# Attention heads on one Trainium2 core: ScalarE takes the second head's exponential of a cell ahead of the first head's

## The chip, the cores and the metric

The kernel runs on one core of a Trainium2 chip. A core has four compute engines that matter here: TensorE (PE in the profile; its weight loads are shown apart as PEld), VectorE (DVE), ScalarE (ACT) and GpSimd (POOL). SyncE (SP) issues transfers. Each engine takes its own list of instructions in order, and engines wait for each other on semaphores. The metric is device time in microseconds (us) of one execution.

## The reference, cut to what matters

The program is a whole block: feed-forward with experts, a wide attention, feed-forward again, a quantized linear layer, an attention with 16 heads, and the linear layer again. The change touches only the attention with 16 heads:

```
q = proj(Wq) / sqrt(DH);  k = proj(Wk);  v = proj(Wv)      # 4 batches, 16 heads, T = 1024, DH = 16
scores = einsum('bhid,bhjd->bhij', q, k)
dist = clip(i[:, None] - i[None, :], 0, 128)
scores = scores + rel[:, dist]                              # a bias by distance
scores = where(i >= j, scores, -inf)                        # causal
y = einsum('bhij,bhjd->bhid', softmax(scores), v)
out = x0 + y.reshape @ Wo.T
```

The bias differs from a constant only where a query lies less than 128 rows behind its key; that strip beside the diagonal, together with the causal mask, is called the band.

## The kernel before

**Units and cells.** The stage "heads" (function `attention_heads`) works through NU = 16 units: 4 batches by 4 groups of HG = 4 heads. A unit is 12 cells (list `CELLS`). A cell is one block j of 128 keys against one half c of the 1024 queries, cut by the causal mask, so that it is 128, 256, 384 or 512 queries wide. Nine of the 12 cells touch the band (`near_of`); they are called near cells here, and the three others, numbers 1, 4 and 7 counted from 0 and all 512 wide, far cells. Over the stage there are 144 near and 48 far cells.

**The four heads of a cell.** A cell has four positions, which hold heads 3, 0, 1 and 2 (`HEAD_OF`). For each position, PE multiplies keys by queries into a PSUM bank (L2316). In a near cell the band is then added: for head 3, at position 0, VectorE adds it in place (L2251); for the other three, PE adds it by two matmuls with an identity (L2320) right behind the score. ScalarE then takes the exponential from the bank into a tile `pt` (L2176). The row maximum is already in the score, as extra rows of the operand. In what follows score 0 to score 3 and exponential 0 to exponential 3 are those of the four positions, and "the add" is VectorE's band of position 0.

**Banks.** The scores of all positions share three PSUM banks in turn (`st_bank`, n % 3, where n counts positions through the stage). Before score n, PE waits until the exponential of n - 3 is done: score 3 of a cell takes the bank of position 0 of the same cell, and scores 0, 1 and 2 take those of positions 1, 2 and 3 of the cell before.

**Values.** The product with v (L2337, eight matmuls a cell) is issued two cells later, behind score 3 of the cell that is then current. It waits for all four exponentials of its own cell.

**What runs in between.** `heads_order` writes one list of steps by hand, and each engine walks it in that order. After each position's score it may place one piece of the row maxima of a later unit: score matmuls into three other banks (L2296) and VectorE's reductions (L2213, L2222, L2225). It also places steps of the next batch's projection (PE, ScalarE L1871 and L1874, VectorE L1903, GpSimd) and the end of the unit before (the transposes and the output projection, L2347, L2355, L2365). The maxima run 1.5 units ahead, so the last unit has none of them beside it. ScalarE has no list of its own: whatever stands in the common list between two positions, such as the projection's copies, stands in its queue there too.

Of the kernel before, what the change touches and what calls it, by code (L numbers as in the profile page):

```python
# [12 lines left out]
ACT = mybir.ActivationFunctionType  # L13
# [16 lines left out]
HG = 4  # L30
NHG = HEADS // HG
HP = HG - 1
# [78 lines left out]
def macaron(nc, x_d, wg_d, w13_d, w2_d, aq_d, ak_d, av_d, fw_d, fb_d, lq_d, lk_d, lv_d, lo_d,  # L111
            rel_d, gamma_d, beta_d, out_d):
    ctx = ExitStack()
    pe, act, dve, pool, sp = nc.tensor, nc.scalar, nc.vector, nc.gpsimd, nc.sync
    uid = [0]

    def sb(stack, name, shape, dt=F32):
        uid[0] += 1
        return stack.enter_context(nc.sbuf_tensor(f"{name}_{uid[0]}", shape, dt))
# [10 lines left out]
    with ctx:  # L130
# [39 lines left out]
        def act_root(at, n):  # L170
            act.wait_ge(*S("variance")(n))
            act.activation(sd[:, at], ve[:, at], ACT.Sqrt).then_inc(*S("root").up())
# [1886 lines left out]
        def attention_heads(tables, ahead):  # L2059
# [8 lines left out]
            NPT = 3 * HG  # L2068
# [4 lines left out]
            score, biased, exped, value, ys_ok = S("score"), S("biased"), S("exp"), S("value"), S("ys")  # L2073
# [16 lines left out]
            near_of = [min((c + 1) * BANK, (j + 2) * P) > max(j * P, c * BANK) for j, c in CELLS]  # L2090
            near_cells = [i for i in range(NCELL) if near_of[i]]

            with ExitStack() as st:
# [9 lines left out]
                pt = [sb(st, f"pt{i}", [P, BANK if i < 2 * HG else 3 * P]) for i in range(NPT)]  # L2103
# [11 lines left out]
                st_bank = lambda n: psum[:, 2 + n % 3, :]  # L2115

                def cell_of(i):

                    u, cell, pos = i
                    j, c = CELLS[cell]  # L2120
                    q0, q1 = max(j * P, c * BANK), (c + 1) * BANK
                    return (u * NCELL + cell) * HG + pos, j, c, HEAD_OF[pos], q0, q1, min(q1, (j + 2) * P)

                def stacks_of(r, u):
                    return S.dma(f"stack_in{r}")(2 * len(SLOTS) * (u // NR + 1))

                def on_sp():
                    for kind, i in order:
                        if kind == "qk" and i % (2 * KD * CB) == 0 and i // (2 * KD * CB) >= 2:
                            b = i // (2 * KD * CB)  # L2130
                            for u in range((b - 1) * NHG - NR, (b - 1) * NHG):
                                sp.wait_ge(*stacks_of(u % NR, u))
                        if kind == "load" and i >= NR:
                            sp.wait_ge(*score((i - NR + 1) * NCELL * HG))
                        ahead.on_sp(kind, i)
                        if kind == "max_out":
                            sp.wait_ge(*max_part(3 * i + 3))
                            sp.dma_start(m_scr[i % 2].rearrange("i c p -> c i p"),
                                         mparts[:, :, :]).then_inc(*S.dma("m_out").up())
                            sp.wait_ge(*S.dma("m_out")(i + 1))  # L2140
                            sp.dma_start(qs[i % NR][KS_ROWS:KS_ROWS + MROWS, :, :].rearrange("i h s -> i (h s)"),
                                         m_scr[i % 2].rearrange("i c p -> i (c p)")
                                         ).then_inc(*S.dma(f"m_in{i % 2}").up())
# [14 lines left out]
                def on_act():  # L2158
                    act_root(LATER, 1)
                    act_root(LATER, 2)  # L2160
                    for kind, i in order:
                        if kind == "v" and i // (2 * CB) >= 2:
                            act.wait_ge(*value((i // (2 * CB) - 1) * NHG * NCELL))
                        if kind == "h_turn" and i >= 2 * KD * CB and i % (KD * CB) == 0:
                            act.wait_ge(*wo_ok(2 * CB * (i // (KD * CB) - 1)))
                        ahead.on_act(kind, i, mx_ring)
                        if kind == "score":
                            n, j, c, h, q0, q1, b1 = cell_of(i)
                            u, cell, pos = i
                            if n >= NPT:  # L2170
                                act.wait_ge(*value(n // HG - 2))
                            if near_of[cell] and h >= HP:
                                act.wait_ge(*biased(u * len(near_cells) + near_cells.index(cell) + 1))
                            else:
                                act.wait_ge(*score(n + 1))
                            act.activation(pt[n % NPT][:, 0:q1 - q0], st_bank(n)[:, 0:q1 - q0],  # L2176
                                           ACT.Exp).then_inc(*exped.up())
                        elif kind == "value":
                            u, cell = i
                            j, c = CELLS[cell]  # L2180
                            if j == LAST[c]:
                                if u:
                                    act.wait_ge(*y_turned(CB * (u - 1) + c + 1))
                                act.wait_ge(*value(u * NCELL + cell + 1))
                                act.activation(ys[:, c * BANK:(c + 1) * BANK], y_banks[c],
                                               ACT.Copy).then_inc(*ys_ok.up())
                        elif kind == "yt_turn":
                            bc, k = divmod(i, KD)
                            if bc:
                                act.wait_ge(*wo_ok(2 * bc))  # L2190
                            act.wait_ge(*ahead.part2(2 * KD * CB * min(bc // CB + 2, BATCH)))
                            act.wait_ge(*yt_turned(i + 1))
                            act.activation(yd[k][:, :], mx_ring.bank((kind, i)), ACT.Copy).then_inc(*yd_ok.up())
# [90 lines left out]
                def on_pe():  # L2284
                    pe.wait_ge(*tables.wo_in)
                    for kind, i in order:
                        ahead.on_pe(kind, i, clear)
                        if kind in ("max_far", "max"):
                            u, h, t = i
# [4 lines left out]
                            if h == 0 and t == QORDER[0]:  # L2294
                                pe.wait_ge(*stacks_of(r, u))
# [7 lines left out]
                        elif kind == "score":  # L2303
                            n, j, c, h, q0, q1, b1 = cell_of(i)
                            u, cell, pos = i
# [4 lines left out]
                                    pe.wait_ge(*zeroed(1))  # L2310
                                pe.wait_ge(*S.dma(f"m_in{u % 2}")(u // 2 + 1))
                            if n >= 3:
                                pe.wait_ge(*exped(n - 2))
                            bank = st_bank(n)
                            by_pe = near_of[cell] and h < HP
                            ins = pe.matmul(bank[:, 0:q1 - q0], ks[r][:, h, j * P:(j + 1) * P], qs[r][:, h, q0:q1],  # L2316
# [7 lines left out]
                        elif kind == "value":  # L2324
                            u, cell = i
                            b, g = divmod(u, NHG)
                            j, c = CELLS[cell]
                            q0 = max(j * P, c * BANK)
# [12 lines left out]
                        elif kind == "y_turn":  # L2341
                            u, t4 = divmod(i, CB)
# [26 lines left out]
                on_sp()  # L2369
                on_pool()  # L2370
                on_act()
                on_dve()
                on_pe()
                end_of_stage("heads")

# [6 lines left out]
        with ExitStack() as stack:  # L2382
            tables = HeadTables(stack)
            ahead = HeadProjection(stack, tables)

            linear(False, (tables, ahead), routing)
            attention_heads(tables, ahead)
# [41 lines left out]
```

## Time and profile before

| what | value |
|---|---|
| median of 3 runs | 2445.11 us (2444.15 to 2449.51) |
| profiled execution | 2448.93 us, its span 2447.2 us |
| heads stage in it, first score to end of the last exponential | 1623.8 to 2347.6 us |
| busy in the whole span | PE 85%, DVE 61%, ACT 39%, POOL 13% |

Busy time of PE is the time from a matmul's start to its modelled end, so that neighbours overlap. An engine's idle time is listed by the instruction that ended it and by what that instruction waited for. PEld idle time may lie under a matmul that is still running.

### The profile page before, as it was taken

The page shows a single profiled execution, that of the slowest core. Times are in us where ns is not written, and L with a number is a line of the kernel's source. Part 1 is how long each engine was busy: PE and PEld are TensorE (multiplying, and loading weights), DVE is VectorE, ACT ScalarE, POOL GpSimd, SP SyncE. Part 2 cuts the span into 40 slices and gives each one's busy share as a digit, 9 for nine tenths or more (in the row PEclk, how much of TensorE's full clock was granted, in tenths as well). Part 3 has the DMA queues.
Part 4 walks back from the last instruction along what each step waited for, and adds up shares of the span by engine and source line. Part 5 has one row for each costly group of instructions (what it writes and reads, how often), then busy time and mean ns, then how long its engine had stood idle before and what let it go on. Part 6 is the DMA issues. An engine that isn't in the chain of part 4 may idle for free.

```text
span 2447.2 us, 38521 instructions
## 1 busy us (share of the span) xinstructions
PE 2071.2 (85%) x12810; PEld 1560.6 (64%) x12810; DVE 1486.5 (61%) x4394; ACT 955.9 (39%) x1944; POOL 308.4 (13%) x300
## 2 busy tenths in 40 slices
PE   4599999976999965999999736478998998999966
PEld 3488888865788944888888625324554455545445
DVE  7754444357455577543434588577776686687548
ACT  4223333322333342233232234325555555655643
POOL 4320000032000043200000242311001101100000
PEclk8799999988999987999999858769999999999988
DMA  8111011011000031201010130433242242333002
GB/s 266 63 61 31 28 30 29 27 50 39 1 1 1 1 108 63 67 28 32 27 32 25 45 90 16 80 51 60 41 53 54 54 53 49 58 43 39 3 9 69
DMA packets 84044, 114.84 MB, mean 47 GB/s; under 512 B 12216, under 2 KB 73824, under 8 KB 80736
## 3 DMA queue, kind: packets, MB, share of 16 engines
q1 hardware_dynamic: 77424, 94.80, 17.8%
q0 software_dynamic: 6432, 17.57, 2.2%
q8 instruction: 113, 1.85, 0.3%
q14 instruction: 75, 0.61, 0.1%
HBM read 69.17 MB, written 43.17 MB: 46 GB/s over the span
## 4 chain that ended last, share of the span: by engine, by line
PE 60%; DVE 26%; issue 4%; ACT 4%; POOL 3%; DMA 2%; SPq 0%; DVEq 0%; ACTq 0%; POOLq 0%
PE psum L811 10%; PE psum L809 10%; PE psum L810 10%; PE psum L126 5%; PE psum L2337 4%; PE psum L128 4%; PE psum L127 4%; DVE mt L2225 4%; PE psum L2316 3%; PE psum L898 3%; DVE m L2213 3%; PE psum L2296 2%; DVE stats L160 2%; DVE m L2222 2%; PE psum L2320 2%
## 5 line engine op out<-in xcount | busy, mean ns | idle before, releaser
L2176 ACT ACTIVATE pt<-psum 128x512 f32<-128x512 f32 (+3 forms) x768 | 333.7, 493 | 275.0 <-DVE psum L2251 180.2
L774 DVE SCALAR_TENSOR_TENSOR h<-psum,xg,sg 128x128 f32<-128x128 f32 x592 | 166.9, 344 | 408.8 <-PE psum L898 404.5
L586 ACT ACTIVATE sg<-psum 128x512 f32<-128x512 f32 x180 | 107.5, 597 | 531.5 <-PE psum L811 531.5
L809 PE MATMUL psum<-w_hi,xt_hi 128*128 (+1 forms) x720 | 288.3, 400 | 5.9 <-DVE xt_lo L739 5.3
L810 PE MATMUL psum<-w_lo,xt_hi 128*128 (+1 forms) x720 | 285.9, 397 | 0.0
L811 PE MATMUL psum<-w_hi,xt_lo 128*128 (+1 forms) x720 | 285.5, 397 | 0.0
L2296 PE MATMUL psum<-ks,qs 96*128 96x512 bf16 (+3 forms) x768 | 235.8, 347 | 44.9 <-DMA ks<-qk_scr 21.9
L2316 PE MATMUL psum<-qs,ks 99*128 99x512 bf16 (+3 forms) x768 | 239.4, 335 | 24.8 <-ACT pt L2176 19.1
L809 PE MATMUL psum<-w_hi,ht_hi 128*128 (+1 forms) x720 | 219.3, 305 | 8.3 <-DVE x L789 8.3
L2225 DVE CUSTOM_DVE_ANT_0 mt<-psum,band_q 128x256 bf16<-128x256 f32 (+1 forms) x512 | 204.7, 400 | 17.8 <-PE psum L2296 7.3
L2320 PE MATMUL psum<-band,ident_r 128*128 128x256 f32 (+1 forms) x864 | 215.1, 338 | 0.0
L811 PE MATMUL psum<-w_hi,ht_lo 128*128 (+1 forms) x720 | 205.1, 285 | 0.0
L810 PE MATMUL psum<-w_lo,ht_hi 128*128 (+1 forms) x720 | 203.8, 283 | 0.0
L2316 PEld LDWEIGHTS psum<-qs,ks 99*128 99x128 bf16 x768 | 68.9, 98 | 189.4 <-ACT pt L2176 112.8
L2213 DVE TENSOR_REDUCE m<-psum 128x1 f32<-128x512 f32 (+1 forms) x256 | 167.0, 652 | 34.5 <-PE psum L2296 30.9
L2337 PE MATMUL psum<-pt,v 128*17 128x512 f32 (+3 forms) x1536 | 162.2, 495 | 0.0
L2320 PEld LDWEIGHTS psum<-band,ident_r 128*128 128x128 f32 x864 | 149.8, 194 | 18.9 <-issue 0.4
L811 PEld LDWEIGHTS psum<-w_hi,xt_lo 128*128 128x128 f32 x720 | 137.8, 191 | 30.3
L809 PEld LDWEIGHTS psum<-w_hi,xt_hi 128*128 128x128 f32 x720 | 138.0, 192 | 29.9 <-issue 5.7
L810 PEld LDWEIGHTS psum<-w_lo,xt_hi 128*128 128x128 f32 x720 | 138.3, 192 | 23.0
L2296 PEld LDWEIGHTS psum<-ks,qs 96*128 96x128 bf16 x768 | 69.3, 99 | 118.5 <-DVE m L2225 45.1
L809 PEld LDWEIGHTS psum<-w_hi,ht_hi 128*128 128x128 f32 x720 | 137.7, 191 | 9.5 <-DVE x L789 9.5
(285 smaller groups left out, 4252.8 us busy)
## 6 DMA issues: line engine op xcount, KB each, us to landing
xg<-w_dram SPq DMA_DIRECT2D x54, 256.0 KB, 3.2
qk_scr<-parts SPq DMA_DIRECT2D x32, 384.0 KB, 2.5
qs<-qk_scr SPq DMA_DIRECT2D x96, 128.0 KB, 7.1
ks<-qk_scr SPq DMA_DIRECT2D x96, 128.0 KB, 7.7
xg<-rows_in SPq DMA_DIRECT2D x74, 132.0 KB, 2.2
rows_out<-yb SPq DMA_DIRECT2D x74, 128.0 KB, 1.7
x<-x_dram SPq DMA_DIRECT2D x4, 1024.0 KB, 8.7
out_dram<-x SPq DMA_DIRECT2D x4, 1024.0 KB, 4.5
```

The costliest lines, as they stand in the source:

```text
L126: pe.matmul(out, ai(ah), bi(bh), start=first, stop=False)
L774: ins = dve.scalar_tensor_tensor(out=h[i % 2][:, e, :], in0=u[:, e, :], scalar=xg[j % XSLOT][:, at:at + 1], in1=sg[i % 2][:, e, :], op0=AL ...
L809: pe.matmul(out, a[0], b[0], start=first, stop=False)
L810: pe.matmul(out, a[0], b[1], start=False, stop=False)
L811: return pe.matmul(out, a[1], b[0], start=False, stop=last)
L2176: act.activation(pt[n % NPT][:, 0:q1 - q0], st_bank(n)[:, 0:q1 - q0], ACT.Exp).then_inc(*exped.up())
L2213: dve.tensor_reduce(m3[u % 2][:, h * BT + t, 0:1], mx_ring.bank((kind, i))[:, 0:cut], AXIS.X, ALU.max).then_inc(*far_max.up())
L2225: dve.tensor_tensor_reduce(junk[:, 0:bw], bank[:, far - cut:w - cut], band_q[:, u % NHG * HG + h, 2 * P - bw:2 * P], 1.0, LOWEST, ALU.add, ...
L2296: pe.matmul(bank[:, 0:c1 - c0], qs[r][0:KS_ROWS, h, t * P:(t + 1) * P], ks[r][0:KS_ROWS, h, c0:c1], start=True, stop=True).then_inc(*(far_ ...
L2316: ins = pe.matmul(bank[:, 0:q1 - q0], ks[r][:, h, j * P:(j + 1) * P], qs[r][:, h, q0:q1], start=True, stop=not by_pe)
L2320: ins = pe.matmul(bank[:, 0:b1 - q0], tables.ident_r[:, :], band[:, part, u % NHG, h, q0 - j * P:b1 - j * P], start=False, stop=(part == 1))
L2337: ins = pe.matmul(y_banks[c][h * MQ:h * MQ + DH + 1, q0 - c * BANK:BANK], v1[b % 2][:, j, g * HG + h, :], slot[:, 0:(c + 1) * BANK - q0], ...
```

## The change

ScalarE's order inside each cell becomes exponential 1, exponential 0, exponential 2, exponential 3, where it was 0, 1, 2, 3. At the step of position 0 it does nothing; at the step of position 1 it takes position 1 and then position 0. Whatever the list places between these two steps now comes ahead of exponential 0. This holds for all 192 cells, near and far. The exponentials are counted by one semaphore in the order in which ScalarE takes them, so PE's wait before a score is rewritten: `exp_rank` says at which rank an exponential is taken. Score 3 waits for rank 2 of its cell (exponential 0, as before), score 0 of the next cell for rank 1 (exponential 1), scores 1 and 2 for ranks 3 and 4. VectorE's and PE's own orders, the banks, and all transfers are as they were.

```
+                def exp_rank(n):
+
+                    return n + (1, -1, 0, 0)[n % HG]
...
                         if kind == "score":
-                            n, j, c, h, q0, q1, b1 = cell_of(i)
                             u, cell, pos = i
-                            if n >= NPT:
-                                act.wait_ge(*value(n // HG - 2))
-                            if near_of[cell] and h >= HP:
-                                act.wait_ge(*biased(u * len(near_cells) + near_cells.index(cell) + 1))
-                            else:
-                                act.wait_ge(*score(n + 1))
-                            act.activation(pt[n % NPT][:, 0:q1 - q0], st_bank(n)[:, 0:q1 - q0],
-                                           ACT.Exp).then_inc(*exped.up())
+                            for pos in ((), (1, 0), (2,), (3,))[pos]:
+                                n, j, c, h, q0, q1, b1 = cell_of((u, cell, pos))
+                                if n >= NPT:
+                                    act.wait_ge(*value(n // HG - 2))
+                                if near_of[cell] and h >= HP:
+                                    act.wait_ge(*biased(u * len(near_cells) + near_cells.index(cell) + 1))
+                                else:
+                                    act.wait_ge(*score(n + 1))
+                                act.activation(pt[n % NPT][:, 0:q1 - q0], st_bank(n)[:, 0:q1 - q0],
+                                               ACT.Exp).then_inc(*exped.up())
...
                             if n >= 3:
-                                pe.wait_ge(*exped(n - 2))
+                                pe.wait_ge(*exped(exp_rank(n - 3) + 1))
```

## Rows read from the trace of the kernel before

**Rows 1.** Chain that ended last, heads stage: share of its time by line.
```profile
by line: PE psum L2337 14.5%; PE psum L2316 11.0%; DVE mt L2225 10.8%; DVE m L2213 7.9%; issue 6.8%; PE psum L2296 6.7%; DVE m L2222 5.8%; PE psum L2320 5.2%; PE psum L126 3.3%; DVE psum L2251 3.0%; ACT pt L2176 2.7%; PE psum L128 2.3%; PE 
```

**Rows 2.** Stretches: length, busy PE, PEld, DVE, ACT, POOL; granted clock, DMA, GB/s.
```profile
1820.00:1880.00 60.00, 51.86 (x321) 30.13 (x321) 40.31 (x139) 31.48 (x69) 9.64 (x8) 1.00 0.21 43
...
2030.00:2060.00 30.00, 25.18 (x152) 13.19 (x151) 19.85 (x68) 15.56 (x35) 7.33 (x6) 0.94 0.05 16
...
1624.00:2350.00 726.00, 667.34 (x4510) 360.18 (x4509) 514.98 (x1859) 413.30 (x920) 59.22 (x56) 0.99 0.27 43
```

**Rows 3.** Line of the exponentials: ScalarE idle before them, then who waited for them (us, times).
```profile
  DVE psum L2251: 180.2, 113
...
  PEld psum L2316: 112.8, 180
  PE psum L2316: 19.1, 43
```

**Rows 4.** Exponentials by shape, heads stage: busy us, mean ns, idle before.
```profile
L2176 ACT ACTIVATE pt<-psum 128x512 f32<-128x512 f32 x384 | 204.8, 600 | 169.9 <-DVE psum L2251 104.6 <-PE psum L2316 55.5 <-PE psum L2320 9.2
```

**Rows 5.** Timeline of a far cell, unit 2, 512 wide: start, length, engine.
```profile
1761.96 0.38 PE L2316 MATMUL psum<-qs,ks 99*128 99x512 bf16 x1
...
1762.11 1.57 ACT L2176 ACTIVATE pt<-psum 128x512 f32<-128x512 f32 x3 [1.55 <-PE psum L2316]
...
1762.76 0.10 PEld L2316 LDWEIGHTS psum<-qs,ks 99*128 99x128 bf16 x1 [0.26 <-ACT pt L2176]
```

**Rows 6.** Timeline of a near cell, unit 2, 512 wide.
```profile
1749.89 0.59 PE L2320 MATMUL psum<-band,ident_r 128*128 128x256 f32 x2
1749.90 0.43 DVE L2251 TENSOR_TENSOR psum<-psum,band_dve 128x256 f32<-128x256 f32 x1 [0.27 <-PE psum L2316]
...
1750.43 1.57 ACT L2176 ACTIVATE pt<-psum 128x512 f32<-128x512 f32 x3 [1.62 <-DVE psum L2251]
...
1751.08 0.39 PE L2316 MATMUL psum<-qs,ks 99*128 99x512 bf16 x1
```

**Rows 7.** Timeline of a near cell, unit 4, 256 wide, with projection beside it.
```profile
1859.97 0.63 ACT L1874 ACTIVATE parts<-rest 128x512 bf16<-128x512 f32 x1 [0.83 <-DVE rest L1903]
...
1860.11 0.27 PE L2316 MATMUL psum<-qs,ks 99*128 99x256 bf16 x1
...
1860.50 0.91 ACT L2176 ACTIVATE pt<-psum 128x256 f32<-128x256 f32 x3
```

**Rows 8.** Timeline of a near cell, unit 8, 256 wide.
```profile
2031.84 0.48 PE L2320 MATMUL psum<-band,ident_r 128*128 128x256 f32 x2
...
2032.92 0.43 DVE L2251 TENSOR_TENSOR psum<-psum,band_dve 128x256 f32<-128x256 f32 x1
...
2033.45 0.94 ACT L2176 ACTIVATE pt<-psum 128x256 f32<-128x256 f32 x3 [3.49 <-DVE psum L2251]
...
2033.89 0.28 PE L2316 MATMUL psum<-qs,ks 99*128 99x256 bf16 x1 [1.21 <-ACT pt L2176]
```

**Rows 9.** Timeline of the second cell of the stage, a far one.
```profile
1629.77 0.61 PE L2316 MATMUL psum<-qs,ks 99*128 99x512 bf16 x1
...
1631.01 0.38 PE L2316 MATMUL psum<-qs,ks 99*128 99x512 bf16 x1
```

**Rows 10.** Timeline of the last cell of the stage, near, 128 wide.
```profile
2346.36 0.67 ACT L2176 ACTIVATE pt<-psum 128x128 f32<-128x128 f32 x3
...
2346.74 0.23 PE L2316 MATMUL psum<-qs,ks 99*128 99x128 bf16 x1 [0.20 <-ACT pt L2176]
```

**Rows 11.** VectorE's add by line, heads stage: busy us, mean ns, idle before.
```profile
L2251 DVE TENSOR_TENSOR psum<-psum,band_dve 128x256 f32<-128x256 f32 x144 | 55.5, 386 | 76.5 <-PE psum L2316 75.8
```

**Rows 12.** Waits of PE and its loads for VectorE's maxima: us, times, longest.
```profile
PEld psum L2296 <- DVE m L2225: 32.8, 87, 0.6
...
PEld psum L2296 <- DVE m L2213: 10.9, 27, 1.3
...
PE psum L2296 <- DVE m L2225: 4.1, 20, 0.3
```

## Prediction

> **What bounds the kernel now.** I read the chain that ended last first. In the heads stage it runs alternately through PE (values, scores, maxima scores) and VectorE (the three reductions of the maxima); the exponentials hold 2.7% of it and VectorE's add 3.0% [rows 1]. The stretch table says the same: of 726 us PE is busy 667, VectorE 515, ScalarE 413 [rows 2]. So ScalarE has room, and PE has little.
>
> Then I read the line of the exponentials. ScalarE stands idle 180.2 us, 113 times, until an add of VectorE's is done [rows 3]. That looks like the thing to remove, but it is idle time of an engine that is not the bound. What counts is who waits for ScalarE in turn: PE itself 19.1 us in 43 cases, PE's weight loads another 112.8 us, most of it under a matmul that still runs [rows 3].
>
> Next I asked for which exponential PE waits, going through the timeline score by score. A score that starts within 0.12 us of the end of the exponential that frees its bank was held by it. Of the 192 scores 3, 102 start so behind exponential 0; the last is that of the last cell [rows 10]. Of the 573 scores 0, 1 and 2 behind their exponentials of the cell before, 11 do. So one edge matters: exponential 0 to score 3. The reader sees it at 1750.43: exponential 0 starts there, takes 0.60 us, and score 3 starts 0.05 us later [rows 4, 6].
>
> **The change, part by part.** Removed and added work: none. There are 768 exponentials before and after, of the same shapes. The waits of scores 0, 1 and 2 change their numbers; exponential 1 then comes earlier, 2 and 3 earlier or later, by one step at most, and as only 11 of those 573 scores were held at all, I book nothing. What covers this is the PE work that stands ahead of those scores (score 3, the values, maxima pieces), which a late exponential 0 holds already. Without that cover it would be one exponential's step, 0.49 us, in those 11 places, 5 us either way.
>
> What moves is exponential 0, and with it score 3. Before, it starts when the add (near cells) or score 0 (far cells) is done. After, it starts when that is so and exponential 1 has been issued, which itself needs score 1. It can never start earlier in its cell than it did. Each exponential behind another costs ScalarE less than its length: three of 512 columns take 1.57 us, one 0.60, so the step is (1.57 - 0.60) / 2 = 0.485 us [rows 4, 5]. From the end of an add to the exponential 0.10 us pass (1749.90 + 0.43 to 1750.43) [rows 6]; I use 0.09 for adds and scores alike.
>
> *Far cells, 48.* There is no add to hide, so the swap only delays. In the cell of [rows 5], score 1 ends at 1761.96 + 0.38 = 1762.34. Exponential 1 starts at 1762.43, exponential 0 at 1762.91, ends at 1763.51, and score 3 starts at 1763.56 instead of 1762.76: 0.80 us late. The second cell of the stage is the first late one: score 1 ends at 1630.38, and score 3 comes at 1630.38 + 0.09 + 0.485 + 0.60 + 0.05 = 1631.60 instead of 1631.01, 0.59 us late [rows 9]. Done for all 48: 41 are late, by 22.8 us together.
>
> *Near cells with nothing else of ScalarE's between positions 0 and 1, 129.* In [rows 6], PE finishes score 1 with its band at 1749.89 + 0.59 = 1750.48, later than the add at 1750.33. Exponential 1 starts at 1750.57, exponential 0 at 1751.06, ends at 1751.66, and score 3 comes at 1751.71 instead of 1751.08: 0.63 us late. Only where the add is very late does the swap cost nothing: in [rows 8] score 1 is done at 2032.32, the add at 2033.35, and exponential 1 fits between; exponential 0 then starts at 2033.45 as before. So it is in 21 of the 144 near cells. Even there score 3 gains nothing, since it waits for exponential 0. Done for all 129: 78 are late, by 23.9 us; the last is the last cell, by about 0.2 us [rows 10].
>
> *Near cells with other work of ScalarE's between the two positions, 15.* Here exponential 0 is moved past that work too. In [rows 7], ScalarE's copy L1874 waits for a projection and for VectorE; the first exponential after it starts at 1860.50. Exponential 0, long done before, would start one step of (0.91 - 0.38) / 2 = 0.27 us later, at 1860.77, and end at 1861.15; score 3 comes at 1861.20 instead of 1860.11, 1.1 us late. Done for the 15: 12 are late, by 13.1 us. The other work gains in return where it stood behind an exponential 0 that waited for its add; the copies there mostly wait for PE, so I book nothing.
>
> The sum is 22.8 + 23.9 + 13.1 = 59.8 us of later scores 3, in 131 cells.
>
> How much of it reaches the end? PE is in order, so behind score 3 stand the values, the next cell's score 0, and every maxima score. VectorE's queue then meets the delay at the next add, which needs score 0. VectorE already stands idle 75.8 us in 62 of its 144 adds for that score [rows 11]; there a delay passes on in full. Taking from each delay the time by which the next cell's add began later than its score allowed leaves 48.1 us. The second cushion is PE's own waiting for the maxima's banks: 32.8 + 10.9 us of load waits, but only 4.1 us of idle matmul time at the larger of the two lines [rows 12]. The cushion is thus between nothing and (32.8 + 10.9) x 131 / 192 = 29.8 us; I take 8, nearer the row of lost matmul time, since load waits lie partly under running matmuls. That leaves 40 us, with ends at 48.1 - 29.8 = 18 and 59.8.
>
> The profiled execution takes 2448.93 us, 3.8 above the median 2445.11. On it the sum gives 2489; on the median 2445.1 + 40 = 2485 us, with 2463 to 2505 as the forecast's own range.
>
> **The rivals.**
>
> *VectorE sets the pace and swallows it.* For it: in stretches of the stage the chain is all VectorE, and the reductions hold 24.5% of it [rows 1]. Against it: VectorE is idle 211 of 726 us [rows 2], a third of that waiting for the very scores that come later. Then only the delays of the last unit, where no maxima run, are sure (4.6 of the 59.8 us), and at most the sum's lower end, 18, is left: 2450 to 2463. The Trainium skill ("Perfetto Trace Analysis", Identifying the Most-Contended Engine) says that busy time of matmuls does not measure PE's headroom and that the engine of highest occupancy is the one to work on; by it VectorE, at 71% here, would be the bound and PE, whose loads are busy 50%, would have room for the delay. The trace bears it out only in part, since scores 3 start right behind exponentials in 102 cells.
>
> *Faster: ScalarE's 180 us were in the way after all.* The mechanism: exponential 1 runs under the add, the cell's four exponentials end sooner, and the banks of exponentials 2 and 3 come free one step earlier, so that PE's stalls on ScalarE shrink. It decides if PE's 19.1 us [rows 3] come from those banks. All of them gone: 2445 - 19 = 2426 us. Against it: 18.3 of the 19.1 us stand before scores 3, which the change cannot bring forward.
>
> *No change.* Gains of this kind and delays cancel, or nearly all delays are swallowed: 2440 to 2450 us. Within 0.2% (4.9 us) is about what a measurement of this kernel can't tell from no change.
>
> *Slower still: PE's clock.* The 1820 to 1880 stretch has PE busy 86% at a full granted clock, but 2030 to 2060, at 84%, has 0.94 [rows 2]: 12% of 30 us, 3.6 us, at 1.2 instead of 2.4 GHz, after PE had stood idle for ScalarE and VectorE. A 512-wide score took 0.61 us at the stage's start and 0.38 one microsecond later [rows 9], so such a fall costs about 0.4 x 3.6 = 1.4 us. If each of the 18 cells with other work between the positions brought one, 25 us come on top: 2510. The Trainium skill ("TensorE: Matmul & The Clock Gate", HAM oscillation) tells of such idling between groups of matmuls that drops PE to half its clock again and again. The trace shows it for stalls longer than most that the change adds.
>
> **How the numbers follow.** Forecast 0.60, clock on top 0.07, swallowed 0.13 (of which 0.02 ends within 0.2%), no change 0.06, faster 0.14. That gives faster 0.14, same 0.08, slower 0.78. The time is the forecast's, 2485. The range for 8 in 10 takes in most of the swallowed case below and the clock case above: 2446 to 2512.
>
> **What the profile after would show.** (1) ScalarE's idle time for the add falls from 180 us to below 60, and its waits for scores grow. (2) PE's idle time and load waits before L2316 grow by 30 us or more, all at score 3. (3) In far cells score 3 starts 0.05 us behind an exponential that started one step behind another. (4) VectorE's idle time before the add grows. (5) The heads stage is some 40 us longer than its 724, and nothing outside it moves. The prediction is wrong if scores 3 are as early as before, or if they are late and the stage isn't; then the cushions were mis-sized.

## The result, and the profile after

The changed kernel takes 2481.83 us in the median (5 runs, 2479.04 to 2486.8) against 2445.11: ratio 1.0146, interval 1.013 to 1.0162, so 36 us slower by the ratio (32 to 40) and 37 between the medians. The forecast was 2485.

The heads stage holds all of it: from the first score to the end of the last exponential it took 723.8 us and takes 759.7 (1619.8 to 2379.5). The rest of the program is 6 us shorter in this profiled execution than in the one before; that reads as scatter of single executions, for the stage's start alone lies anywhere from 1619.8 to 1626.4 us in the traces of the kernels shown here. The stretch table of the changed kernel (length; busy PE, PEld, DVE, ACT, POOL; clock) for that stage, and the chain that ended last in it, by line:

```profile
1619.80:2379.50 759.70, 666.96 (x4488) 358.76 (x4492) 517.01 (x1857) 420.94 (x919) 59.19 (x56) 0.99 0.26 41
```

```profile
by line: PE psum L2342 16.1%; PE psum L2321 15.1%; ACT pt L2181 9.4%; issue 8.7%; PE psum L2301 8.5%; PE psum L2325 7.6%; DVE mt L2230 4.6%; DVE m L2218 3.6%; PE psum L126 2.9%; PE psum L2370 2.9%; DVE m L2227 2.5%; PE psum L128 2.2%; PE ps
```

Busy times of PE and VectorE are those of [rows 2] within some 2 us (ScalarE's is 8 us longer); what has grown is the idle time. On the chain the exponentials rose from 2.7% to 9.4% and the three reductions of the maxima fell from 24.5% to 10.7% [rows 1]: what PE waits for has moved from VectorE to ScalarE. (Lines have moved by five: L2181 is the exponential, L2321 the score, L2325 PE's band, L2256 VectorE's add, L2301 the maxima's scores, L2342 the values.)

The waits of the changed kernel (who waits for whom; us in total, times, longest), in a view that begins at 1624, four microseconds into the stage, and so lacks VectorE's and ScalarE's first waits:

```profile
PEld psum L2321 <- ACT pt L2181: 174.1, 230, 3.4
ACT pt L2181 <- PE psum L2325: 173.7, 240, 2.5
...
DVE psum L2256 <- PE psum L2321: 84.2, 62, 6.0
PE psum L2321 <- ACT pt L2181: 64.1, 120, 3.2
ACT pt L2181 <- PE psum L2321: 57.4, 46, 1.9
...
PEld psum L2301 <- DVE m L2230: 14.7, 55, 0.6
...
PEld psum L2301 <- DVE m L2218: 9.1, 20, 1.1
...
ACT pt L2181 <- DVE psum L2256: 6.4, 16, 2.6
```

The whole run's line of the exponentials (busy, mean ns, idle before them and what ended it), before and after:

```profile
L2176 ACT ACTIVATE pt<-psum 128x512 f32<-128x512 f32 (+3 forms) x768 | 333.7, 493 | 275.0 <-DVE psum L2251 180.2 <-PE psum L2316 55.5 <-PE psum L2320 32.8
...
L2181 ACT ACTIVATE pt<-psum 128x512 f32<-128x512 f32 (+3 forms) x768 | 341.8, 490 | 279.0 <-PE psum L2325 211.6 <-PE psum L2321 57.4 <-DVE psum L2256 6.4
```

The 180.2 us that ScalarE waited for the add [rows 3] are down to 6.4. They are not saved: ScalarE's waits for PE's band, that is, for score 1, grew from 32.8 to 211.6 us, and all its idle time before exponentials is 279.0 us where it was 275.0. (Some 37 us of either sum are its one wait for the stage to begin.) PE's idle time before scores rose from 19.1 to 64.1 us, its load waits there from 112.8 to 174.1. At the same time PE's load waits for the maxima's banks fell from 43.7 [rows 12] to 23.8 us.

The same far cell as in [rows 5], score 0 in the timeline before and then the timeline of the changed kernel:

```profile
1761.62 0.39 PE L2316 MATMUL psum<-qs,ks 99*128 99x512 bf16 x1
...
1760.79 0.39 PE L2321 MATMUL psum<-qs,ks 99*128 99x512 bf16 x1
...
1761.13 0.38 PE L2321 MATMUL psum<-qs,ks 99*128 99x512 bf16 x1
...
1761.60 2.22 ACT L2181 ACTIVATE pt<-psum 128x512 f32<-128x512 f32 x4 [1.64 <-PE psum L2321]
1761.67 0.38 PE L2321 MATMUL psum<-qs,ks 99*128 99x512 bf16 x1
...
1762.74 0.10 PEld L2321 LDWEIGHTS psum<-qs,ks 99*128 99x128 bf16 x1 [1.08 <-ACT pt L2181]
1762.74 0.39 PE L2321 MATMUL psum<-qs,ks 99*128 99x512 bf16 x1 [0.69 <-ACT pt L2181]
```

Score 1 ends at 1761.51, ScalarE starts 0.09 us later, and score 3 comes 1762.74 - 1760.79 = 1.95 us after score 0, where it came 1.14 after (1761.62 to 1762.76): 0.81 us late, worked out as 0.80. PE stands idle 0.69 us for it. The near cell of [rows 6], again score 0 before and then the changed kernel:

```profile
1749.47 0.39 PE L2316 MATMUL psum<-qs,ks 99*128 99x512 bf16 x1
...
1747.20 0.39 PE L2321 MATMUL psum<-qs,ks 99*128 99x512 bf16 x1
...
1747.62 0.59 PE L2325 MATMUL psum<-band,ident_r 128*128 128x256 f32 x2
1747.63 0.43 DVE L2256 TENSOR_TENSOR psum<-psum,band_dve 128x256 f32<-128x256 f32 x1 [0.27 <-PE psum L2321]
...
1748.31 1.57 ACT L2181 ACTIVATE pt<-psum 128x512 f32<-128x512 f32 x3 [1.78 <-PE psum L2325]
...
1749.45 0.39 PE L2321 MATMUL psum<-qs,ks 99*128 99x512 bf16 x1 [0.50 <-ACT pt L2181]
```

The add is done at 1748.06, but ScalarE starts at 1748.31, behind PE's band of score 1 (1748.21). Score 3 comes 2.25 us after score 0 and not 1.61 (1749.47 to 1751.08): 0.64 us late, worked out as 0.63.

Adding this up over all cells, from the starts of scores in the two timelines:

| cells | score 0 to score 3, before, after | worked out | score 3 to next score 0, before, after |
|---|---|---|---|
| 45 far, no other ScalarE work between | 71.7, 94.4: +22.7 us | +22.8 | 45.9, 42.5: -3.4 us |
| 129 near, none between | 263.5, 285.0: +21.5 | +23.9 | 209.0, 201.4: -7.6 |
| 15 near, with other work between | 56.6, 65.9: +9.3 | +13.1 | 53.9, 46.7: -7.2 |
| together | +53.5 | +59.8 | -18.2 |

The loss is the difference, 35.3 of the 35.9 us by which the stage grew; the three far cells with other ScalarE work, left out here, add 0.4. In the last unit, where no maxima run, nothing is given back: from its first to its last score it took 30.0 us and takes 34.8, +4.8 where 4.6 had been worked out. That is closer than it should be: 1.1 of the 4.8 us lie in its first cell, where the rule of the far and near cells gives some 0.5. That cell began at half the clock (the stretch 2342 to 2346 has a granted clock of 0.57), where before the whole unit ran at 1.00.

### The profile page after: what moved, and what is told of

It reads as the page before. It is cut to its first block, busy times and chain, and to the rows that moved or that the text cites. A ratio compares the mean times of both kernels' runs of the same rounds, so it can differ in the third digit from the quotient of the medians.

```text
span 2477.3 us, 38521 instructions
## 1 busy us (share of the span) xinstructions
PE 2068.3 (83%) x12810; PEld 1554.9 (63%) x12810; DVE 1486.2 (60%) x4394; ACT 964.1 (39%) x1944; POOL 308.0 (12%) x300
## 4 chain that ended last, share of the span: by engine, by line
PE 62%; DVE 20%; ACT 6%; issue 5%; POOL 3%; DMA 2%; SPq 0%; ACTq 0%; DVEq 0%; POOLq 0%
PE psum L811 9%; PE psum L809 9%; PE psum L810 9%; PE psum L2342 5%; PE psum L2321 5%; PE psum L126 4%; PE psum L128 4%; PE psum L127 4%; PE psum L898 3%; ACT pt L2181 3%; PE psum L2301 3%; PE psum L2325 2%; DVE mt L2230 2%; DVE stats L160 2%; DVE m L2218 1%
## 5 line engine op out<-in xcount | busy, mean ns | idle before, releaser
L2181 ACT ACTIVATE pt<-psum 128x512 f32<-128x512 f32 (+3 forms) x768 | 341.8, 490 | 279.0 <-PE psum L2325 211.6
L2321 PE MATMUL psum<-qs,ks 99*128 99x512 bf16 (+3 forms) x768 | 239.7, 334 | 70.7 <-ACT pt L2181 64.1
L2301 PE MATMUL psum<-ks,qs 96*128 96x512 bf16 (+3 forms) x768 | 230.8, 345 | 38.4 <-DMA ks<-qk_scr 22.2
L2321 PEld LDWEIGHTS psum<-qs,ks 99*128 99x128 bf16 x768 | 68.3, 97 | 249.6 <-ACT pt L2181 174.4
L2325 PE MATMUL psum<-band,ident_r 128*128 128x256 f32 (+1 forms) x864 | 217.2, 338 | 0.0
L2218 DVE TENSOR_REDUCE m<-psum 128x1 f32<-128x512 f32 (+1 forms) x256 | 167.0, 652 | 43.1 <-PE psum L2301 39.4
L2325 PEld LDWEIGHTS psum<-band,ident_r 128*128 128x128 f32 x864 | 150.3, 195 | 18.8 <-issue 0.7
L2342 PE MATMUL psum<-pt,v 128*17 128x512 f32 (+3 forms) x1536 | 161.2, 493 | 0.0
L810 PEld LDWEIGHTS psum<-w_lo,xt_hi 128*128 128x128 f32 x720 | 137.2, 190 | 22.8
L810 PEld LDWEIGHTS psum<-w_lo,ht_hi 128*128 128x128 f32 x720 | 138.3, 192 | 0.0
```

The lines of the kernel that those rows point to most:

```text
L810: pe.matmul(out, a[0], b[1], start=False, stop=False)
L2218: dve.tensor_reduce(m3[u % 2][:, h * BT + t, 0:1], mx_ring.bank((kind, i))[:, 0:cut], AXIS.X, ALU.max).then_inc(*far_max.up())
L2301: pe.matmul(bank[:, 0:c1 - c0], qs[r][0:KS_ROWS, h, t * P:(t + 1) * P], ks[r][0:KS_ROWS, h, c0:c1], start=True, stop=True).then_inc(*(far_ ...
L2325: ins = pe.matmul(bank[:, 0:b1 - q0], tables.ident_r[:, :], band[:, part, u % NHG, h, q0 - j * P:b1 - j * P], start=False, stop=(part == 1))
L2342: ins = pe.matmul(y_banks[c][h * MQ:h * MQ + DH + 1, q0 - c * BANK:BANK], v1[b % 2][:, j, g * HG + h, :], slot[:, 0:(c + 1) * BANK - q0], ...
```

## The experiments

Two theories were put against each other. Bank theory: score 3 needs the bank that exponential 0 frees, and that comes later. ScalarE theory: the loss lies in ScalarE's own queue, whichever bank is freed.

**The swap in some cells only.** Four kernels differ from the changed one by where `swapped` holds; elsewhere the cell keeps the old order:

```
+                            for pos in ((), (1, 0), (2,), (3,))[pos] if swapped(u * NCELL + cell) else (pos,):
# near_only: near_of[m % NCELL]      far_only: not near_of[m % NCELL]
# late_only: m in (21 cells)         not_beside: m not in (18 cells)
```

Near cells only. 

> The swap in the 144 near cells alone; far cells keep exponential 0 first. Bank theory (the loss is score 3 waiting for a bank that a later exponential 0 frees): first-order delay 37.0 of the 59.8 us, and at the 0.61 of it that the changed kernel showed, +23 us over the kernel before (+15 to +30). Rival, ScalarE theory (the loss lies in ScalarE's own queue, which stands waiting for score 1 wherever there is no add to hide): the near cells have an add to hide, so here +0 to +10.

Measured: 2470.18 us, ratio 1.0086 (1.007 to 1.0102): +21 us.

Far cells only. 

> The swap in the 48 far cells alone. Bank theory: first-order delay 22.8 us, at 0.61 of it +14 us (+8 to +20). Rival, ScalarE theory: nearly the whole loss of the change sits here, +27 to +37. Rival, VectorE swallows it: +0 to +5.

Measured: 2463.5 us, ratio 1.0077 (1.0063 to 1.0092): +19 us. The two parts add up to the whole within their intervals. Neither holds nearly all of it, so it is not a matter of having no add to hide under; and the far cells' share is not swallowed.

The 21 cells with the latest adds. 

> The swap in only those 21 near cells where the add came so late that exponential 1 fits ahead of it. Bank theory: score 3 still waits for exponential 0 at the same time, exponentials 2 and 3 end one step sooner but nothing waits for them: same within 5 us (-3 to +4). Rival, ScalarE's idle time was in the way: these cells hold its longest waits, and one step of 0.2 to 0.49 us in 21 cells shows as -4 to -10 us.

Measured: 2449.1 us, ratio 1.0005 (0.9996 to 1.0014). ScalarE's longest waits can be filled with exponential 1 (its waits for the add fell from 180.2 to 160.5 us), and nothing comes of it.

All but the cells with other ScalarE work. 

> The changed order in all cells but the 18 in which other work of ScalarE's stands between positions 0 and 1 (15 near, 3 far). By the prediction's third term these hold 13.1 of 59.8 us of later scores 3; at 0.61 of it the loss shrinks from 37 to +29 us against the kernel before (+24 to +34). Rival: those cells' other work gains as much as score 3 loses there (copies no longer stand behind an exponential that waits for its add), so the loss stays at 37 or grows.

Measured: 2480.06 us, ratio 1.014 (1.0125 to 1.0156): +34 us (31 to 38). That can't be told from the full change, and it lies at the upper end of what had been expected. In the 15 near cells the third term of the sum was there (+9.3 us until score 3), but 7.2 us of it were given back before the next score 0, as the table above shows. So those cells cost some 2 us and not 8. Whether the copies' gain gave it back, as the rival says, or the cushions did, no run separates.

**Only the wait.** ScalarE's order as before; PE waits longer before score 3:

```
-                                pe.wait_ge(*exped(n - 2))
+                                pe.wait_ge(*exped(n - 1 if n % HG == HG - 1 else n - 2))
```

> ScalarE's order as in the kernel before; only PE's wait before score 3 asks for exponential 1 of the cell as well as exponential 0. Nothing else moves. Bank theory: score 3 would start 50.3 us later in sum over the cells of the kernel before (38.5 near, 11.8 far), at 0.61 of it +31 us (+20 to +40). ScalarE theory: ScalarE's queue is untouched, so +0 to +6.

Measured: 2485.96 us, ratio 1.0153 (1.0138 to 1.0167): +37 us. The waits of that kernel:

```profile
ACT pt L2176 <- DVE psum L2251: 182.8, 116, 36.9
...
PE psum L2316 <- ACT pt L2176: 55.4, 100, 3.5
```

ScalarE's idle time for the add is as before the change, yet the loss is as large as the change's. In its trace score 0 to score 3 takes 47.8 us more over the stage than before, where 50.3 had been worked out, and 11.4 of them come back before the next score 0. So a later score 3 is enough to make a loss of this size.

**Four banks for the scores.** With either order of exponentials, four PSUM banks go round the scores and two remain for the maxima and the projection. PE's wait before score n then asks for the exponential of n - 4:

```
-            mx_ring = Ring([u for u in order if u[0] in MX], [psum[:, 5 + i, :] for i in range(3)])
+            mx_ring = Ring([u for u in order if u[0] in MX], [psum[:, 6 + i, :] for i in range(2)])
-                st_bank = lambda n: psum[:, 2 + n % 3, :]
+                st_bank = lambda n: psum[:, 2 + n % 4, :]
...
-                            if n >= 3:
-                                pe.wait_ge(*exped(n - 2))
+                            if n >= 4:
+                                pe.wait_ge(*exped(n - 3))              # new order: exped(exp_rank(n - 4) + 1)
```

Old order. 

> The kernel before with four PSUM banks for scores in turn and two, not three, for the maxima and projection ring. Score 3 then takes the bank of position 3 of the cell before, and no score waits for an exponential of its own cell. Its time by itself is open: 18 us of PE's stalls at score 3 go, two banks in place of three cost an unknown amount on the maxima; -10 to +60 us. It is the base for the next kernel.

Measured: 2541.21 us, ratio 1.0392 (1.0375 to 1.0409): +96 us, outside the -10 to +60 that had been given for it.

New order. 

> The same four and two banks with the changed order of exponentials. Bank theory: with the bank wait gone the changed order costs nothing, within 8 us of the kernel with four banks and the old order. ScalarE theory: the changed order costs 25 to 40 us here too.

Measured: 2540.56 us, ratio 1.0393 (1.0376 to 1.041). The order of exponentials costs nothing here. The pair is weaker evidence than it looks, though: with two banks the maxima set the pace, as the waits of the old order show, and PE has room to spare:

```profile
PE psum L2296 <- DVE m L2213: 21.9, 48, 2.9
PE psum L2296 <- DVE m L2225: 18.8, 68, 0.4
...
PE psum L2316 <- ACT pt L2176: 1.5, 1, 1.5
```

The last unit, which has no maxima, is the cleaner pair. From its first to its last score it takes 26.1 us with the old order and 26.8 with the new, +0.7 where three banks made it +4.8.

Giving the third bank of the maxima and the projection to the scores costs some 96 us net. Not all of that need be waiting for banks: the granted clock over the stage is 0.96 with the old order and 0.97 with the new, where it was 0.99 before, and no run separates the two.

**Cover for the wait.** The values of the cell two back go ahead of score 3, with either order:

```
                     for pos in range(HG):
+                        if pos == HG - 1 and len(due) > 1:
+                            yield due.pop(0)
                         yield [("score", (u, cell, pos))]
                     due.append([("value", (u, cell))])
-                    if len(due) > 2:
-                        yield due.pop(0)
```

Old order. 

> The kernel before with the product with v of the cell two back placed ahead of score 3, where it stood behind it. PE then has 0.4 to 1.0 us of work while exponential 0 runs. Bank theory: most of the 18.3 us of PE's stalls at score 3 go, -5 to -20 us against the kernel before. ScalarE theory: the stalls at score 3 don't bind, same within 5 us.

New order. 

> The product with v ahead of score 3, and the changed order of exponentials. Bank theory: the later exponential 0 is mostly covered, 0 to 12 us above the same placement with the old order, where the change alone costs 37. ScalarE theory: 25 to 40 us above it.

Measured: 2458.67 us, ratio 1.005 (1.0033 to 1.0067), with the old order, and 2456.18 us, ratio 1.0038 (1.0026 to 1.0051), with the new. Under the cover the order makes no difference that can be measured, as bank theory has it; in the last unit it is 29.4 us with the old order and 30.1 with the new. But the old order lost 12 us where both theories expected none or a gain. The waits of the kernel with the values ahead and the old order:

```profile
DVE m L2213 <- PE psum L2296: 54.8, 71, 4.2
DVE psum L2251 <- PE psum L2316: 53.3, 33, 4.5
...
DVE m L2222 <- PE psum L2296: 22.4, 27, 2.1
...
PE psum L2316 <- ACT pt L2176: 9.5, 25, 2.2
```

PE's stalls for ScalarE are halved, but VectorE's waits for the maxima's scores rose from 30.9 and 9.5 us to 54.8 and 22.4, while its wait for the add's score fell from 75.8 [rows 11] to 57.7 (53.3 in this view, which lacks the stage's first). Together that is 19 us more idle time of VectorE's at these three lines, for a loss of 12. Why the maxima's scores reach VectorE later is not settled by a run.

**The other way round: an earlier exponential 0.** Head 3 moves to position 1 or 2, so that the add runs under exponential 0 and score 3 no longer hangs on it:

```
-        HEAD_OF = (HG - 1, *range(HG - 1))
+        HEAD_OF = (0, HG - 1, *range(1, HG - 1))      # add_second
+        HEAD_OF = (0, 1, HG - 1, 2)                   # add_third
```

> ScalarE's order as in the kernel before, but head 3, whose band VectorE adds, sits at position 1 and not 0. The add then runs under exponential 0, which needs no VectorE, and score 3 waits for that exponential alone. Bank theory: score 3 is held less often and for less, -8 to -25 us against the kernel before. Rival: PE now adds the band to position 0, and its two matmuls (0.24 us) plus the later score 1 make up for it, same within 5 us.

> The same with head 3 at position 2. The add has two exponentials to run under, but exponential 2 and with it 3 may stand waiting for it, and score 1 of the next cell takes that bank. Bank theory: exponential 0 is free of the add here too, so as much as with position 1, -8 to -25 us. Rival: as before, same within 5 us.

Measured: 2446.36 us, ratio 0.9999 (0.9991 to 1.0008), and 2445.5 us, ratio 0.9997 (0.9988 to 1.0006): no gain, where 8 to 25 us were expected. The waits with head 3 at position 1:

```profile
PEld psum L2296 <- DVE m L2225: 48.1, 124, 0.6
...
PEld psum L2296 <- DVE m L2213: 20.0, 42, 2.5
...
PE psum L2296 <- DVE m L2225: 8.1, 31, 0.3
...
PE psum L2296 <- DVE m L2213: 7.8, 16, 2.3
...
PE psum L2316 <- ACT pt L2176: 6.0, 19, 1.6
```

The stalls before scores went as expected, from 19.1 to 6.0 us: over the stage, score 0 to score 3 takes 15.1 us less. But 11.1 us of that come back between score 3 and the next score 0, where PE waits for VectorE instead. Its load waits for the maxima's banks rose from 43.7 to 68.1 us. PE gets to the next maxima score sooner and finds the bank still full. In the last two units (first score to first score, and first to last), where few or no maxima run, the gain is there: 32.9 and 28.5 us against 33.9 and 30.0.

**A thinner add.** To see whether it is VectorE's work that takes the gain back, VectorE adds one column only, and the rest of head 3's bias and mask is left out:

```
-                                at = st_bank(n)[:, 0:b1 - q0]
+                                at = st_bank(n)[:, 0:1]
...
```

> The kernel before, with VectorE adding one column of the band instead of 128 or 256: the rest of head 3's bias and causal mask is left out. The waits stay. Exponential 0 comes some 0.3 us earlier in near cells, as it did with head 3 at position 1 (which gave nothing), and VectorE has some 45 of its 515 us less to do. If VectorE's work on the maxima takes back what an earlier score 3 gives, the relief shows here: -15 to -45 us. If the add's work lies in VectorE's idle time and the earlier score 3 gives nothing, 0 to -5 us.

Measured: 2431.25 us, ratio 0.9928 (0.991 to 0.9946): -18 us (13 to 22). VectorE's add in this kernel (compare [rows 11]) and PE's waits before its scores:

```profile
L2251 DVE TENSOR_TENSOR psum<-psum,band_dve 128x1 f32<-128x1 f32 x144 | 23.6, 164 | 76.4 <-PE psum L2316 75.8
```

```profile
PE psum L2316 <- ACT pt L2176: 11.6, 26, 2.9
```

The adds take 23.6 us where they took 55.5, so VectorE has 32 us less to do and not the 45 that had been expected. Score 0 to score 3 takes 15.1 us less over the stage, just as much less as with head 3 at position 1. But here nothing comes back between score 3 and the next score 0 (another 1.5 us are gained), where there it was 11.1. So an earlier score 3 pays when VectorE's load is lighter too, and is taken back when it is not. The one run doesn't separate VectorE's maxima from its adds.

## Why the prediction was right, step by step

*The edge.* That only exponential 0 to score 3 matters held. In the changed kernel PE's idle time for exponentials lies before scores 3 (23.3 us in far and 40.0 in near cells, of 64.1); scores 0, 1 and 2 are held in 4 places instead of 11. The kernel with nothing changed but that wait lost as much as the change.

*The three terms.* Far cells 22.8 us against 22.7 measured; near cells without other work 23.9 against 21.5; near cells with other work 13.1 against 9.3. One rule made all three: score 1, a step of ScalarE's, exponential 0, score 3. The cells where the add is late enough cost nothing, as forecast: in the cell of [rows 8], score 3 comes 2.19 us after score 0 and came 2.20.

*The cushions.* Their sum was right, and that was partly luck. The prediction took 11.7 us for adds that VectorE began late anyway and 8 for PE's own waits at the maxima's banks, 19.7 together; 18.2 were given back. But the 8 was a choice between nothing and 29.8, and the return was uneven: 3.4 of 22.7 us in the far cells, 7.6 of 21.5 in the near ones, and 7.2 of 9.3 beside other ScalarE work, whose gain the prediction had booked at nothing. How the 18.2 split isn't settled either. PE's load waits for the maxima's banks shrank by 43.7 - 23.8 = 19.9 us, but such waits lie in part under running matmuls; between scores 3 and the next scores 0 PE's own idle time fell by 9 us only (12.9 to 3.9). VectorE met the delay less at the add (its idle time there rose by 13 us, 75.8 to 88.7 over the whole stage) than at the maxima, whose two lines of waits rose from 30.9 and 9.5 to 39.4 and 25.8.

*The rivals.* "Faster" fell with the 21 latest cells: their waits were filled and the time stayed. "VectorE swallows it" can account for a third of the delay at most, the 18.2 of 53.5 us that were given back. The clock stayed out of it: 0.99 over the stage before and after, in spite of more stalls (120 before scores where there were 43). The Trainium skill's account of such idling ("TensorE: Matmul & The Clock Gate", HAM oscillation) is not shown by this change. The Trainium skill's rule on the engine to work on ("Perfetto Trace Analysis", Identifying the Most-Contended Engine), which points at VectorE, agrees with the runs where something was to be gained (the thinner add paid, the earlier score 3 alone didn't), and not where something was lost: two thirds of PE's delay went through.

*What the prediction didn't see.* It judged the kernel by what a later score 3 costs. An earlier one was worth nothing as long as VectorE had all its work. The waits suggest why: PE and VectorE are nearly in step, so that a delay of PE's passes to VectorE's next add or maximum, while a gain of PE's ends at a bank that VectorE has not emptied. None of the kernels that keep the computation whole beats the kernel before.

## What to carry to other kernels

A long idle time of an engine off the chain (180 us here) says little; ask which instruction the next engine in the chain waits for, and whether a new order makes that one earlier or later. Where a bank goes round among a few users, taking another user's result first delays the one whose bank is due next. And where two engines run nearly in step, delays and gains are not mirror images: check what the engine would wait for next before counting a removed stall as time.

## What the runs showed of the hardware

PE's idle time in the stage rose from 58 us (723.8 - 665.4 busy) to 93 us (759.7 - 667.0), most of it in stalls before scores of up to 3.2 us, and its granted clock over the stage stayed at 0.99. More stalls did not bring more falls of the clock: before, it was down at 1.2 GHz in two places of the stage (0.66 in the stretches 1674 to 1679 and 2039 to 2044), after, in one (0.57 from 2342 to 2346). The kernels with four banks for the scores did run at a lower clock, 0.96 and 0.97 over the stage; what brought it down stays open.
